# Expert routing tables of a state-space/mixture-of-experts kernel: part of their making moved into the convolution, the sums on two column positions of TensorE

## The chip, the cores and the metric

The kernel runs on one core of a Trainium2 chip. The metric is the device time of one launch in microseconds (us), the median of the runs. Engines: TensorE (PE, matmuls and its weight loads PEld), VectorE (DVE), ScalarE (ACT), GpSimd (POOL), and SyncE (SP), which here only issues DMAs.

## The reference

`x` has 32 sequences of 64 channels and 1024 time steps. A state-space convolution along time (its kernel made from `log_dt`, `C`, `A`; a skip `D`; a length mask) gives 2048 token rows of 1024 numbers. A mixture of 16 experts follows, two experts to a token, and its output is added to `x`:

```python
y = irfft(rfft(u * mask) * rfft(kernel))[..., :L] + u * mask * D   # then * mask
probs = softmax(y @ gate_w.T); vals, idx = top_k(probs, 2); vals /= vals.sum(-1)
h = silu(y @ g.T) * (y @ u.T)                  # 16 experts of 112
out = x + einsum('bei,hei,be->bh', h, d, w)    # w: vals at idx, else 0
```

All is fp32.

## The kernel before, in words

**Convolution.** The 64 channels are taken in 16 groups (`G`) of 4 (`HG`). For each group VectorE copies the new convolution kernel out of PSUM (`kernel_rows`), SyncE stores it to `k_rows` in DRAM and reads it back as Toeplitz matrices (L303, L312); TensorE runs 8 matmuls for each channel (`convolve_channel`, L939); VectorE reads each channel's result with the mask (`outputs`, L727) and transposes it to blocks (`block_rows`), and ScalarE issues the store of these as token rows of `y_rows` (`rows_out`). One group later TensorE makes the gate products on four column positions (`gates`, L950), ScalarE copies them (`partials`, L532), a matmul folds them to the logits of 128 tokens (`route`, L959), and VectorE copies these (`router`, L742). So a group is also a group of 128 tokens.

**Routing.** Every (choice k, group g) column of 128 tokens gets a slot in a list sorted by expert, in tiles of 128 slots. `choose` (L744) finds the two best experts of each token and one-hots of them, for 14 groups inside the last group of the convolution and for 2 behind it. Then two matmuls count tokens before and within the groups (L1023, L1024), VectorE scans them (L816), waits for ScalarE's exponentials (`spread_exp`), works out weights, tile starts and slots (L822 to L846), and in five `PIECES` the one-hot of a slot's tile (48 columns, `slot_hot`, L852) and of its row in the tile (128 columns, `slot_row`, L855). GpSimd multiplies the tile one-hot by the token's number and by its weight (L429, L432). TensorE sums 32 products `slot_row^T x [token part | weight part]` into one table (L1033: 128x128 against 96 columns). VectorE turns its first half into `from_row` (L860 to L862), the second into `slot_weight` (L864), and then works out each tile's expert (L866 to L875). `stay_awake` runs matmuls without use between these steps.

**Tiles.** GpSimd gathers 128 rows of `y_rows` per tile by `from_row` (L441; eight tiles ahead), then issues four empty scatters (L472). For each tile TensorE turns the rows (L1061), ScalarE and VectorE copy them, TensorE multiplies by gate and up weights (L1052), by the down weights (L1071), VectorE and ScalarE weigh the result (L906, L582), and GpSimd scatters it with addition into `out` (L456), which holds a copy of `x`. SyncE keeps six experts' weights in a ring: experts 0 to 2, then two pieces of the copy of `x`, then 3 to 5 are issued right behind the last Toeplitz loads; from 6 on as tiles finish.

Each engine runs its own queue in program order; semaphores order the engines.

Of the kernel before, what the change touches and what calls it, by code (L numbers as in the profile page):

```python
# [6 lines left out]
B, H, L = 32, 64, 1024  # L7
N = 64
P = 128
# [31 lines left out]
PIECES = ((0, 4), (4, 8), (8, 16), (16, 24), (24, K * G))  # L41
# [4 lines left out]
def build(nc, x_time, x_rows, lengths, params, skip, gate_t, gu_t, d_t, out):  # L46
# [4 lines left out]
    with ctx:  # L51
# [27 lines left out]
        at += 2 * HG * L - K * G * (P + 3 * MC)  # L79
        slot_row = flat[:, at:at + K * G * P].rearrange("p (j r) -> p j r", j=K * G)  # L80
        at += K * G * P
        slot_tile = flat[:, at:at + 2 * K * G * MC].rearrange("p (j n) -> p j n", j=K * G)
        at += 2 * K * G * MC
        slot_hot = flat[:, at:at + K * G * MC].rearrange("p (j n) -> p j n", j=K * G)
        par = sb("par", [P, 5, H])
# [46 lines left out]
        not_first = sb("not_first", [P, E, G])  # L132
        run = sb("run", [P, E, G])
# [3 lines left out]
        dest = sb("dest", [P, E, G])  # L137
        slot = sb("slot", [P, K * G])
# [16 lines left out]
        ys_of = [ys[:, s, :] for s in range(RY - R)] + [ys_more[:, s, :] for s in range(R)]  # L155
# [6 lines left out]
        k_bank = pb("k_bank", [P, HG, LO])  # L162
        k_ps = k_bank[0:LO, :, :]
        later_ps = conv_ps[:, 0, 0:E * G].rearrange("p (e g) -> p e g", e=E)
        count_ps = conv_ps[:, 1, 0:E * G].rearrange("p (e g) -> p e g", e=E)
        table_ps = conv_ps[:, 2, 0:2 * MC]
# [58 lines left out]
        hot_row_made = sem("hot_row_made")  # L225
        hot_weight_made = sem("hot_weight_made")
        hot_token_made = sem("hot_token_made")
        sources_made = sem("sources_made")
        table_made = sem("table_made")
# [42 lines left out]
        def _(sp):  # L272
# [66 lines left out]
        def _(pool):  # L339
# [68 lines left out]
            link(nc.gpsimd.memset(not_first[:, :, :], 1.0))  # L408
            nc.gpsimd.memset(not_first[:, :, 0:1], 0.0).then_inc(starts_marked, 1)
# [15 lines left out]
            weights = weight[:, :, :].rearrange("p k g -> p (k g)")  # L425
            for q, (lo, hi) in enumerate(PIECES):
                js = slice(lo, hi)
                pool.wait_ge(hot_made, q + 1)
                nc.gpsimd.tensor_tensor(slot_tile[:, js, 0:MC], slot_hot[:, js, :],  # L429
                                        token_no[:, js].unsqueeze(2).to_broadcast([P, hi - lo, MC]),  # L430
                                        ALU.mult).then_inc(hot_token_made, 1)
                nc.gpsimd.tensor_tensor(slot_tile[:, js, MC:], slot_hot[:, js, :],  # L432
                                        weights[:, js].unsqueeze(2).to_broadcast([P, hi - lo, MC]),
                                        ALU.mult).then_inc(hot_weight_made, 1)

# [28 lines left out]
            pool.wait_ge(ys_cleared, 2)  # L464
            for t in range(RY):
                gather(t)
# [31 lines left out]
        def _(act):  # L498
# [57 lines left out]

# [4 lines left out]

            nc.scalar.activation(silu[:, 0, 0:1], len_f[:, 0:1], ACT.Silu)

# [35 lines left out]
        def _(dve):  # L599
# [119 lines left out]
            def outputs(g, p, first):  # L719
# [5 lines left out]
                for h in range(HG):  # L725
                    dve.wait_ge(conv_done, g * HG + h + 1)
                    nc.vector.tensor_tensor(y_t[:, p, h, :, :],  # L727
                                            conv_ps[:, h, 0:C * B].rearrange("p (c b) -> p c b", c=C),
                                            mask_t[:, :, :], ALU.mult).then_inc(conv_read, 1)

# [13 lines left out]
            def choose(lo, hi):  # L744

                for g in range(lo, hi):
                    nc.vector.max(top_v[:, g, :], logits[:, g, :]).then_inc(top_found, 1)
                dve.wait_ge(top_found, hi)
                for g in range(lo, hi):
                    nc.vector.max_index(top_i[:, g, :], top_v[:, g, :], logits[:, g, :]).then_inc(top_made, 1)  # L750
                dve.wait_ge(top_made, hi)
# [8 lines left out]

                tt(spread[:, lo:hi, :], logits[:, lo:hi, :], top_v[:, lo:hi, 0:1].to_broadcast([P, n, E]), ALU.subtract)
# [3 lines left out]


# [22 lines left out]
            with dve.Fori(1, (G - 4) // 2) as i:  # L789
                for p in range(2):  # L790
# [4 lines left out]
                    angles(2 * i + 4 + p, p, False)  # L795
            for g in range(G - 4, G):
                if g + 2 < G:
                    kernel_rows(g + 2, g % 2, (g + 2) // 2, False)
                if g == G - 1:

                    dve.wait_ge(log_made, G - 2)
                    choose(0, G - 2)
                outputs(g, g % 2, False)
# [7 lines left out]
            choose(G - 2, G)  # L811
            block_rows(G - 1, (G - 1) % 2, (G - 1) // 2, False)

            dve.wait_ge(starts_marked, 1)
            dve.wait_ge(counted, 1)
            link(nc.vector.tensor_tensor_scan(run[:, :, :].rearrange("p e g -> p (e g)"),  # L816
                                              not_first[:, :, :].rearrange("p e g -> p (e g)"),
                                              conv_ps[:, 1, 0:E * G], 0.0, ALU.mult, ALU.add))


            dve.wait_ge(spread_exp, 1)
            links(vec.tensor_scalar(tiles[:, :], run[:, :, G - 1], 1.0 / P, HALF_DOWN, ALU.mult, ALU.add),  # L822
                  vec.reduce_sum(total[:, :], spread[:, :, :], AX.X))
            links(vec.tensor_scalar(tiles[:, :], tiles[:, :], ROUND, ROUND, ALU.add, ALU.subtract),
                  vec.reciprocal(total[:, :], total[:, :]))
            links(vec.tensor_scalar(tiles[:, :], tiles[:, :], 1.0, None, ALU.max, ALU.bypass),
                  vec.tensor_tensor(weight[:, :, :], top2[:, :, :], total[:, :].unsqueeze(1).to_broadcast([P, K, G]),
                                    ALU.mult))
            links(vec.tensor_tensor_scan(ends[:, :], ones[:, 0:E], tiles[:, :], 0.0, ALU.mult, ALU.add),
                  vec.tensor_tensor(norm[:, :], weight[:, 0, :], weight[:, 1, :], ALU.add))  # L830
            vec.tensor_copy(ends_i[:, :], ends[:, :]).then_inc(ends_made, 1)
            links(vec.tensor_tensor(starts[:, :], ends[:, :], tiles[:, :], ALU.subtract),
                  vec.reciprocal(norm[:, :], norm[:, :]))


            links(vec.tensor_tensor(weight[:, :, :], weight[:, :, :], norm[:, :].unsqueeze(1).to_broadcast([P, K, G]),
                                    ALU.mult),
                  vec.tensor_tensor(dest[:, :, :], run[:, :, :], later_ps, ALU.add))
            stt(dest[:, :, :], starts[:, :].unsqueeze(2).to_broadcast([P, E, G]), float(P), dest[:, :, :],
                ALU.mult, ALU.add)  # L840
            links(*[nc.vector.tensor_tensor(chosen[:, k, :, :], chosen[:, k, :, :],
                                            dest[:, :, :].rearrange("p e g -> p g e"), ALU.mult) for k in range(K)])
            link(nc.vector.reduce_sum(slot[:, :], chosen[:, :, :, :].rearrange("p k g e -> p (k g) e"), AX.X))
            ts(slot_q[:, :], slot[:, :], 1.0 / P, -HALF_DOWN, ALU.mult, ALU.add)
            ts(slot_q[:, :], slot_q[:, :], ROUND, ROUND, ALU.add, ALU.subtract)
            stt(slot[:, :], slot_q[:, :], -float(P), slot[:, :], ALU.mult, ALU.add)  # L846


            for q, (lo, hi) in enumerate(PIECES):
                js = slice(lo, hi)  # L850
                col = [P, hi - lo, MC]
                nc.vector.tensor_tensor(slot_hot[:, js, :], slot_q[:, js].unsqueeze(2).to_broadcast(col),  # L852
                                        iota_row[:, 0:MC].unsqueeze(1).to_broadcast(col),
                                        ALU.is_equal).then_inc(hot_made, 1)
                nc.vector.tensor_tensor(slot_row[:, js, :], slot[:, js].unsqueeze(2).to_broadcast([P, hi - lo, P]),  # L855
# [275 lines left out]
```

## Time and profile before

| | us |
|---|---|
| median of 3 runs (lowest, highest) | 499.8 (499.45, 500.56) |
| the profiled execution | 496.27 |
| its span, first to last instruction | 494.2 |
| TensorE busy | 435.8 (88%) |
| VectorE / ScalarE / GpSimd busy | 195.8 / 100.9 / 177.6 |

The span in 40 equal slices of 12.4 us; a digit is the busy share in tenths, PEclk the granted clock of TensorE in tenths of full speed, DMA the mean share of 16 DMA engines:

```profile
PE   0359999989999998895969999999999999999991
...
DVE  6924344333444432639613333333333333333330
ACT  3870000000001000011012222222222232222220
POOL 4542332222222200005685334446344354552322
PEclk9989999999999999997899999999999999999997
DMA  8966898989889998899584897997997796775541
```

The first 17 slices are the convolution, slices 18 to 20 (counted from 1) the routing, the rest the tiles. How to read it: an engine's share over the whole span mixes these stages; what counts for the change is what ended each wait in the middle one.

### The profile page before, as it was taken

The page shows a single profiled execution, that of the slowest core. Times are in us where ns is not written, and L with a number is a line of the kernel's source. Part 1 is how long each engine was busy: PE and PEld are TensorE (multiplying, and loading weights), DVE is VectorE, ACT ScalarE, POOL GpSimd, SP SyncE. Part 2 cuts the span into 40 slices and gives each one's busy share as a digit, 9 for nine tenths or more (in the row PEclk, how much of TensorE's full clock was granted, in tenths as well). Part 3 has the DMA queues.
Part 4 walks back from the last instruction along what each step waited for, and adds up shares of the span by engine and source line. Part 5 has one row for each costly group of instructions (what it writes and reads, how often), then busy time and mean ns, then how long its engine had stood idle before and what let it go on. Part 6 is the DMA issues. An engine that isn't in the chain of part 4 may idle for free.

```text
span 494.2 us, 9023 instructions
## 1 busy us (share of the span) xinstructions
PE 435.8 (88%) x2834; PEld 381.2 (77%) x2834; DVE 195.8 (40%) x512; ACT 100.9 (20%) x229; POOL 177.6 (36%) x217
## 2 busy tenths in 40 slices
PE   0359999989999998895969999999999999999991
PEld 0359998879899898884958887888887788888770
DVE  6924344333444432639613333333333333333330
ACT  3870000000001000011012222222222232222220
POOL 4542332222222200005685334446344354552322
PEclk9989999999999999997899999999999999999997
DMA  8966898989889998899584897997997796775541
GB/s 282 341 204 191 283 265 269 287 261 276 279 284 304 306 295 261 284 387 350 151 299 86 261 285 169 277 273 205 285 250 209 213 278 154 152 159 97 86 71 20
DMA packets 46490, 115.98 MB, mean 235 GB/s; under 512 B 10098, under 2 KB 25714, under 8 KB 46322
## 3 DMA queue, kind: packets, MB, share of 16 engines
q1 hardware_dynamic: 25138, 73.49, 45.5%
q0 software_dynamic: 12096, 33.58, 29.8%
q10 hardware_dynamic: 9216, 8.39, 5.5%
q8 instruction: 23, 0.38, 0.3%
q14 instruction: 17, 0.14, 0.1%
HBM read 93.63 MB, written 40.66 MB: 272 GB/s over the span
## 4 chain that ended last, share of the span: by engine, by line
PE 58%; DMA 23%; SPq 6%; DVE 6%; issue 2%; POOL 2%; ACT 0%; another core or an unknown queue 0%; ACTq 0%; POOLq 0%; DVEq 0%
PE conv_ps L1052 25%; DMA k_rows<-k_sb 17%; PE conv_ps L1071 14%; PE conv_ps L939 9%; PE turn_ps L1061 7%; DMA arena<-k_rows 4%; SPq L312 4%; SPq L311 3%; PE conv_ps L1033 2%; DVE tmp L622 1%; DMA ys<-y_rows,from_row 1%; PE conv_ps L1078 1%; POOL arena L429 1%; PE turn_ps L950 1%; DMA out<-arena,from_row 1%
## 5 line engine op out<-in xcount | busy, mean ns | idle before, releaser
L939 PE MATMUL conv_ps<-arena 128*128 128x256 f32 (+7 forms) x1024 | 157.1, 310 | 12.7 <-DMA arena<-k_rows 12.3
L939 PEld LDWEIGHTS conv_ps<-arena 128*128 128x128 f32 x1024 | 148.8, 192 | 20.6 <-issue 8.5
L1052 PE MATMUL conv_ps<-arena,ys_t 128*128 x640 | 127.8, 353 | 3.8 <-DVE ys_t L886 3.8
L1052 PEld LDWEIGHTS conv_ps<-arena,ys_t 128*128 128x128 f32 x640 | 118.1, 190 | 15.5 <-issue 15.5
L456 POOL DMA_INDIRECT out<-arena,from_row x40 | 62.9, 1572 | 119.9 <-DMA out<-arena,from_row 82.3
L1071 PE MATMUL conv_ps<-arena,hid_t 112*128 x160 | 75.7, 595 | 1.0 <-DVE hid_t L901 1.0
L727 DVE TENSOR_TENSOR arena<-conv_ps,mask_t 128x256 f32<-128x256 f32 x64 | 27.0, 424 | 98.6 <-PE conv_ps L939 97.7
L894 DVE TENSOR_TENSOR hid<-silu,conv_ps 128x112 f32<-128x112 f32 x40 | 10.9, 272 | 102.1 <-ACT silu L576 98.4
L906 DVE TENSOR_SCALAR arena<-conv_ps,slot_weight 128x512 f32<-128x512 f32 x40 | 30.0, 751 | 42.7 <-PE conv_ps L1071 41.7
L385 POOL TENSOR_TENSOR am<-wave,cs_re 128x128 f32<-128x128 f32 x16 | 6.5, 406 | 108.8 <-ACT wave L518 105.4
L1071 PEld LDWEIGHTS conv_ps<-arena,hid_t 112*128 112x128 f32 x160 | 27.2, 190 | 21.0 <-issue 20.8
L582 ACT ACTIVATE arena<-conv_ps,slot_weight 128x512 f32<-128x512 f32 x40 | 27.5, 688 | 47.3 <-PE conv_ps L1071 46.2
L886 DVE COPY ys_t<-turn_ps 128x512 f32<-128x512 f32 x40 | 27.7, 692 | 16.6 <-PE turn_ps L1061 13.4
L569 ACT COPY ys_t<-turn_ps 128x512 f32<-128x512 f32 x40 | 23.4, 586 | 51.4 <-PE turn_ps L1061 47.0
L576 ACT ACTIVATE silu<-conv_ps 128x112 f32<-128x112 f32 x40 | 10.6, 264 | 100.5 <-PE conv_ps L1052 98.1
L518 ACT ACTIVATE wave<-angle 128x384 f32<-128x384 f32 x16 | 8.2, 521 | 109.2 <-DVE angle L672 109.2
L429 POOL TENSOR_TENSOR arena<-arena,token_no 128x384 f32<-128x384 f32 (+1 forms) x5 | 7.3, 1451 | 54.5 <-DVE arena L852 54.5
L988 PE MATMUL turn_ps<-ones 128*128 128x128 f32 x50 | 7.6, 313 | 20.0 <-DVE cs_im L707 20.0
L441 POOL DMA_INDIRECT ys<-y_rows,from_row x20 | 21.3, 1064 | 9.7 <-issue 5.8
L441 POOL DMA_INDIRECT arena<-y_rows,from_row x20 | 21.0, 1050 | 6.1 <-issue 6.1
L1061 PE MATMUL turn_ps<-ident,ys 128*128 128x128 f32 x160 | 20.8, 273 | 1.8 <-DMA ys<-y_rows,from_row 1.8
L988 PEld LDWEIGHTS turn_ps<-ones 128*128 128x128 f32 x50 | 6.9, 222 | 20.0 <-issue 19.9
(149 smaller groups left out, 369.6 us busy)
## 6 DMA issues: line engine op xcount, KB each, us to landing
arena<-k_rows SPq DMA_DIRECT2D x64, 512.0 KB, 6.6
arena<-gu_t SPq DMA_DIRECT2D x16, 896.0 KB
y_rows<-y_blk ACTq DMA_DIRECT2D x64, 128.0 KB, 3.1
arena<-x_time SPq DMA_DIRECT2D x56, 128.0 KB, 5.3
arena<-d_t SPq DMA_DIRECT2D x16, 448.0 KB
arena<-x_time SPq DMA_DIRECT2D x2, 512.0 KB, 6.0
out<-arena,from_row POOLq DMA_INDIRECT x44
out<-ys SPq DMA_DIRECT2D x1, 512.0 KB, 7.4
```

The source lines that it names most:

```text
L312: sp.dma_start(toep[:, p, h, :], bass.AP(k_rows, (g * HG + h) * KROW, [[1, P], [1, L]])).then_inc(toep_in[p][h], 16)
L441: nc.gpsimd.indirect_dma_start(out=ys_of[t % RY], out_offset=None, in_=y_rows, in_offset=bass.IndirectOffsetOnAxis(ap=from_row[:, t:t + 1] ...
L456: nc.gpsimd.indirect_dma_start(out=out, out_offset=bass.IndirectOffsetOnAxis(ap=from_row[:, t:t + 1], axis=0), in_=od[:, t % R, :], in_off ...
L569: nc.scalar.copy(ys_t[:, t % 2, 0:C // 2, :], ytr_ps[:, 0:L // 2].rearrange("p (c n) -> p c n", n=P)).then_inc(yst_act, 1)
L582: nc.scalar.mul(od[:, t % R, 0:L // 2], down_ps[:, 0, :], slot_weight[:, t:t + 1]).then_inc(od_act, 1)
L727: nc.vector.tensor_tensor(y_t[:, p, h, :, :], conv_ps[:, h, 0:C * B].rearrange("p (c b) -> p c b", c=C), mask_t[:, :, :], ALU.mult).then_i ...
L886: nc.vector.tensor_copy(ys_t[:, t % 2, C // 2:, :], ytr_ps[:, L // 2:].rearrange("p (c n) -> p c n", n=P)).then_inc(yst_dve, 1)
L906: nc.vector.tensor_scalar(od[:, t % R, L // 2:], down_ps[:, 1, :], slot_weight[:, t:t + 1], None, ALU.mult, ALU.bypass).then_inc(od_dve, 1)
L939: last = nc.tensor.matmul(conv_ps[:, h, d * B:C * B], toep[:, p, h, d * P:(d + 1) * P], u_t[:, p, h, 0:(C - d) * B], start=(d == 0), stop= ...
L1052: last = nc.tensor.matmul(gu_ps, ys_t[:, t % 2, c, :], flat[:, bass.ds(bufs[t] * WE + c * GU, GU)], start=(c == 0), stop=(c == C - 1))
L1061: last = nc.tensor.transpose(ytr_ps[:, c * P:(c + 1) * P], ys_of[t % RY][:, c * P:(c + 1) * P], ident[:, :])
L1071: last = nc.tensor.matmul(down_ps[:, n, :], hid_t[:, t % 2, :], flat[0:INTER, bass.ds(bufs[t] * WE + C * GU + n * (L // 2), L // 2)], star ...
```

## The change

Groups 0 to 11 (`GA` = 12) are handled apart from groups 12 to 15 (`GB` = 4). What happens to the early ones goes between the channels of the last three groups of the convolution. A slot is now split: the rank of a token among its expert's tokens gives the row in the tile without the tile starts; the tile is the start plus the quotient of the rank.

Row one-hots of the early groups are multiplied by the token number by ScalarE (`token_rows`), ahead of and behind the last `partials`. Each table is summed as `tile one-hot^T x row one-hot`, 48 columns of weights against 128 columns, even columns at position 0 and odd ones at 64, copied by ScalarE to `halves`, and folded and turned by one matmul. There are two tables, one behind the other: tokens (with `from_row` and the first four gathers right behind) and weights. `slot_row` now lies in the buffers of gathered tiles 4 to 7, `row_token` over weights of experts 3 to 5, whose loads go behind the token table. The exponentials move ahead of the last `rows_out`, the weights behind the slots.

```diff
-            sp.wait_ge(factors_made, G)
-            load_expert(3)
-            load_expert(4)
-            sp.wait_ge(conv_done, G * HG)
-            load_expert(5)
-            for e in range(WB):
-                sp.wait_ge(w_in[e % WB], 32)
+            for e in range(3):
+                sp.wait_ge(w_in[e], 32)
+                sp.sem_inc(weights_ready, 1)
+            sp.wait_ge(tokens_out, 1)
+            for e in range(3, WB):
+                load_expert(e)
+            for e in range(3, WB):
+                sp.wait_ge(w_in[e], 32)
                 sp.sem_inc(weights_ready, 1)
...
+            pool.wait_ge(hot_made, 2 * K)
+            for k in range(K):
+                js = slice(k * G + GA, (k + 1) * G)
+                nc.gpsimd.tensor_tensor(hot_token[:, k * GB:(k + 1) * GB, :], slot_hot[:, js, :],
+                                        token_no[:, js].unsqueeze(2).to_broadcast([P, GB, MC]),
+                                        ALU.mult).then_inc(late_tokens, 1)
...
-            for t in range(RY):
+            for t in range(R):
+                gather(t)
+            pool.wait_ge(weights_out, 1)
+            for t in range(R, RY):
                 gather(t)
...
+            def token_rows(q):
+                k, lo = q // 2, (q % 2) * HALF
+                act.wait_ge(rows_made, q + 1)
+                for j in range(k * G + lo, k * G + lo + HALF):
+                    last = nc.scalar.mul(row_token[:, j, :], slot_row[:, j, :], token_no[:, j:j + 1])
+                last.then_inc(row_tokens, 1)
...
+            act.wait_ge(factors_made, G)
+            for q in range(3):
+                token_rows(q)
             partials(G - 1, (G - 1) % 2, False)
-            rows_out(G - 1, (G - 1) % 2)
+            token_rows(3)
             act.wait_ge(spread_made, 2)
...
+            rows_out(G - 1, (G - 1) % 2)
...
+            for n in range(2):
+                act.wait_ge(halves_summed[n], 1)
+                for part in (slice(0, MC), slice(P // 2, P // 2 + MC)):
+                    nc.scalar.copy(halves[part, n, :], halves_ps[n][part, :]).then_inc(halves_copied[n], 1)
...
+            between = {
+                G - 4: (None,) * HG,
+                G - 3: (lambda: best(0, GA), lambda: best_at(0, HALF), lambda: best_at(HALF, GA), None),
+                G - 2: (lambda: choose(0, GA), lambda: spreads(0, GA), None, None),
+                G - 1: (early_ranks, early_rows, more_rows, None),
+            }
...
+            rows_of(1, HALF, GA)
             router(G - 1, (G - 1) % 2)
...
+            for k in range(K):
+                hot_of(k, 0, GA)
+            for k in range(K):
+                hot_of(k, GA, G)
+            for k in range(K):
+                rows_of(k, GA, G)
+            dve.wait_ge(spread_exp, 1)
...
+            dve.wait_ge(tokens_out, 1)
...
+            for k in range(K):
+                js = slice(k * G, (k + 1) * G)
+                vec.tensor_tensor(hot_weight[:, js, :], slot_hot[:, js, :],
+                                  weights[:, js].unsqueeze(2).to_broadcast([P, G, MC]), ALU.mult).then_inc(weighted, 1)
...
+            dve.wait_ge(weights_out, 1)
+            nc.vector.tensor_copy(slot_weight[:, :], weight_ps).then_inc(lists_made, 1)
...
+                    if h == 3 and counting:
+                        pe.wait_ge(chosen_made, 1)
+                        pe.wait_ge(k_copied, G)
+                        count_tokens(later_a, count_a, slice(0, GA))
...
+            pe.wait_ge(ranks_begun, 1)
+            stay_awake(6, k_bank[:, 0:P])
             pe.wait_ge(chosen_made, 2)
+            count_tokens(later_b, count_b, slice(GA, G))
+            stay_awake(29, k_bank[:, 0:P])
+            def half_table(n, j, hot, row, first, last):
+                part = slice((j % 2) * (P // 2), (j % 2) * (P // 2) + MC)
+                return nc.tensor.matmul(halves_ps[n][part, :], hot, row, start=first, stop=last)
+            for n, (j, late) in enumerate(COLS):
+                if late:
+                    pe.wait_ge(late_tokens, j // G + 1)
+                    pe.wait_ge(rows_made, 2 * K + j // G + 1)
+                    hot, row = hot_token[:, (j // G) * GB + j % G - GA, :], slot_row[:, j, :]
+                else:
+                    pe.wait_ge(hot_made, j // G + 1)
+                    pe.wait_ge(row_tokens, 2 * (j // G) + (j % G) // HALF + 1)
+                    hot, row = slot_hot[:, j, :], row_token[:, j, :]
+                last = half_table(0, j, hot, row, n < 2, n >= last_two)
+            last.then_inc(halves_summed[0], 1)
+            stay_awake(2, k_bank[:, 0:P])
+            pe.wait_ge(halves_copied[0], 2)
+            nc.tensor.matmul(token_ps, halves[:, 0, :], fold_tiles[:, :], start=True, stop=True).then_inc(tokens_out, 1)
+            stay_awake(4, k_bank[:, 0:P])
+            for j in range(K * G):
+                pe.wait_ge(weighted, j // G + 1)
+                last = half_table(1, j, hot_weight[:, j, :], slot_row[:, j, :], j < 2, j >= last_two)
+            last.then_inc(halves_summed[1], 1)
+            pe.wait_ge(halves_copied[1], 2)
+            nc.tensor.matmul(weight_ps, halves[:, 1, :], fold_tiles[:, :], start=True, stop=True).then_inc(weights_out, 1)
+            stay_awake(4, k_bank[:, 0:P])
```

In order, the pieces are of SyncE, GpSimd (two), ScalarE (three), VectorE (four) and TensorE. `COLS` names the 24 early columns first. `early_ranks` scans the early counts and multiplies them with the chosen one-hots, `early_rows` reduces these to ranks, takes them modulo 128 and makes the first six row one-hots (`rows_of`), `more_rows` twelve more. GpSimd also makes `fold_tiles` and clears `halves` and two masks at the start of the kernel.

## Rows read from the trace of the kernel before

**Rows 1.** Chain of waits, 213 to 270: start us, length us, what.

```profile
213.26 0.43 DVE arena L727
...
220.38 1.28 ACT L559
...
234.35 7.55 PE conv_ps L1033 x48
...
242.41 0.20 DVE from_row L862
...
243.57 4.59 DMA ys<-y_rows,from_row
...
248.21 1.11 PE turn_ps L1061 x8
...
254.20 2.25 another core or an unknown queue
...
267.32 1.72 PE conv_ps L1071 x4
```

**Rows 2.** Stage windows: length, busy us (instructions) of each engine, PEclk, DMA share, GB/s.

```profile
230.00:232.00 2.00, 2.00 (x10) 2.00 (x11) 2.00 (x3) 0.00 (x0) 2.00 (x3) 0.50 1.02 345
...
255.00:260.00 5.00, 2.58 (x14) 2.58 (x15) 0.89 (x2) 0.59 (x1) 4.08 (x4) 1.00 0.65 252
```

**Rows 3.** TensorE's timeline: start, busy us, line; records are two a matmul.

```profile
202.92 2.48 PE L939 MATMUL conv_ps<-arena 128*128 128x256 f32 x16 [1.55 <-DMA arena<-k_rows]
...
213.74 0.65 PE L950 MATMUL turn_ps<-arena,gate_w 128*32 128x128 f32 x16 [0.52 <-DVE arena L727]
...
217.89 6.86 PE L988 MATMUL k_bank<-ones 128*128 128x128 f32 x60
229.79 3.70 PE L1033 MATMUL conv_ps<-arena 128*128 128x96 f32 x16 [5.05 <-POOL arena L432]
```

**Rows 4.** GpSimd's timeline: its first factors, and one product with token numbers.

```profile
19.89 0.40 POOL L385 TENSOR_TENSOR am<-wave,cs_re 128x128 f32<-128x128 f32 x1 [3.47 <-DVE cs_im L707]
...
229.66 0.95 POOL L429 TENSOR_TENSOR arena<-arena,token_no 128x192 f32<-128x192 f32 x1
```

**Rows 5.** ScalarE: timeline, and its group of scaled 512-column copies on the page.

```profile
14.34 7.74 ACT L502 ACTIVATE arena<-steps,decay 128x64 f32<-128x64 f32 x32
...
214.45 0.27 ACT L532 COPY parts<-turn_ps 128x128 f32<-128x128 f32 x1 [8.13 <-PE turn_ps L950]
...
L582 ACT ACTIVATE arena<-conv_ps,slot_weight 128x512 f32<-128x512 f32 x40 | 27.5, 688 | 47.3 <-PE conv_ps L1071 46.2
```

**Rows 6.** VectorE's timeline, 203 to 243.

```profile
203.21 1.17 DVE L747 MAX8 top_v<-logits 128x8 f32<-128x16 f32 x14
...
215.20 0.18 DVE L742 COPY logits<-turn_ps 128x16 f32<-128x16 f32 x1 [1.43 <-PE turn_ps L959]
...
218.23 0.65 DVE L816 TENSOR_TENSOR_SCAN run<-not_first,conv_ps 128x256 f32<-128x256 f32 x1
222.32 0.17 DVE L822 TENSOR_SCALAR tiles<-run 128x16 f32<-128x16 f32 x1 [3.44 <-ACT top L560]
...
226.41 0.69 DVE L843 TENSOR_REDUCE slot<-chosen 128x32 f32<-128x512 f32 x1
...
228.07 0.68 DVE L855 TENSOR_TENSOR arena<-slot,iota_row 128x512 f32<-128x512 f32 x1
...
229.25 0.99 DVE L855 TENSOR_TENSOR arena<-slot,iota_row 128x512 f32<-128x512 f32 x1
...
242.76 0.95 DVE L616 TENSOR_TENSOR passed<-iota_row,ends 128x768 f32<-128x768 f32 x1
```

**Rows 7.** DMA queues in 232 to 234, then 245 to 258: packets, MB, share.

```profile
q1 hardware_dynamic: 129, 0.62, 84.5%
q10 hardware_dynamic: 127, 0.11, 19.4%
...
q0 software_dynamic: 1187, 4.01, 87.4%
```

More of the change, by code:

```diff
@@ L40 @@
 SPANS = ((0, USUAL), (USUAL, USUAL + 4), (USUAL + 4, MT))
-PIECES = ((0, 4), (4, 8), (8, 16), (16, 24), (24, K * G))
+GA = G - 4
+GB = G - GA
+HALF = GA // 2
+COLS = tuple((k * G + g, 0) for k in range(K) for g in range(GA)) + tuple(
+    (k * G + g, 1) for k in range(K) for g in range(GA, G))
 NONE = 4 * K * TOK
@@ L154, in build @@
         ys = sb("ys", [P, RY - R, L])
-        ys_of = [ys[:, s, :] for s in range(RY - R)] + [ys_more[:, s, :] for s in range(R)]
+        slot_row = ys[:, :, :].rearrange("p s n -> p (s n)").rearrange("p (j r) -> p j r", j=K * G)
+        ys_of = [ys_more[:, s, :] for s in range(R)] + [ys[:, s, :] for s in range(RY - R)]
         ys_t = sb("ys_t", [P, 2, C, P])
@@ L717, in kernel_rows, with outputs @@
                                         ALU.add).then_inc(k_added, 1)
-            def outputs(g, p, first):
+            def outputs(g, p, first, between=(None,) * HG):
                 if not first:
@@ L806, in _ @@
                 router(g - 1, (g - 1) % 2)
+            rows_of(1, HALF, GA)
             router(G - 1, (G - 1) % 2)
             dve.wait_ge(log_made, G)
-            choose(G - 2, G)
+            best(GA, G)
+            best_at(GA, G)
+            choose(GA, G)
+            spreads(GA, G)
             block_rows(G - 1, (G - 1) % 2, (G - 1) // 2, False)
[L814 to L818, printed above, removed]
@@ L821, in _ @@
-            dve.wait_ge(spread_exp, 1)
-            links(vec.tensor_scalar(tiles[:, :], run[:, :, G - 1], 1.0 / P, HALF_DOWN, ALU.mult, ALU.add),
-                  vec.reduce_sum(total[:, :], spread[:, :, :], AX.X))
+            dve.wait_ge(counted, 2)
+            link(vec.tensor_tensor_scan(run_b[:, :, :].rearrange("p e g -> p (e g)"),
+                                        not_first_b[:, :, :].rearrange("p e g -> p (e g)"),
+                                        count_b, 0.0, ALU.mult, ALU.add))
@@ L836, in _ @@
+            link(vec.reciprocal(norm[:, :], norm[:, :]))
             links(vec.tensor_tensor(weight[:, :, :], weight[:, :, :], norm[:, :].unsqueeze(1).to_broadcast([P, K, G]),
                                     ALU.mult),
[L838 to L855, printed above, removed]
-                                        iota_row[:, :].unsqueeze(1).to_broadcast([P, hi - lo, P]),
-                                        ALU.is_equal).then_inc(hot_row_made, 1)
@@ L974, in convolve_first, with count_tokens, convolve @@
                         route(0, 0, True)
-            def convolve(g, p, i, second=False):
+            def count_tokens(later, count, groups):
+                nc.tensor.matmul(later, not_before[:, :], both[:, :, groups], start=True, stop=True)
+                nc.tensor.matmul(count, ones[:, :], both[:, :, groups], start=True, stop=True).then_inc(counted, 1)
+            def convolve(g, p, i, second=False, counting=False):
                 for h in range(HG):
+                    if h == 3 and counting:
+                        pe.wait_ge(chosen_made, 1)
+                        pe.wait_ge(k_copied, G)
+                        count_tokens(later_a, count_a, slice(0, GA))
                     pe.wait_ge(toep_in[p][h], 32 * i + 16)
@@ L1012, in _ @@
             for g in range(G - 4, G):
-                convolve(g, g % 2, g // 2)
+                convolve(g, g % 2, g // 2, counting=g == G - 2)
                 if g + 3 < G:
```

178 lines of the change are left out of this document (117 added, 61 removed).

## The prediction

> **What bounds the kernel now.** I read the chain of waits first. Between the convolution and the expert tiles it leaves TensorE's useful work: the last convolution result is read at 213.26, the first gathered tile is turned at 248.21, and from there to the end the chain is one 5.73 us tile after another (down projection at 261.59, then 267.32) [rows 1]. So 34.95 us lie in the routing stretch, and whatever brings the turn at 248.21 forward comes off the end, as long as the tiles keep their pace. The chain's pieces there are the exponentials (table load at 220.38), the table matmuls (234.35, 7.55 us for 24 of the 32), the cast of the sources (242.41) and the first gather (243.57, landing in 4.59 us). After it there is one odd piece, 2.25 us at 254.20 that the profile ascribes to nothing it knows. Then the stage windows: in 230 to 232 the granted clock is 0.50, the 1.2 GHz level, so the table matmuls run at half speed; TensorE had waited 5.05 us before them [rows 2, 3]. In 255 to 260 it is busy for 2.58 of 5 us and the clock is 1.00 [rows 2].
>
> **Part 1: the work put into the convolution.** Counting 12 groups on TensorE adds two matmuls over 192 columns before the last channel of group 14, some 0.7 us. Group 15 then waits 1.55 us for its Toeplitz rows anyway [rows 3], so I cost it at nothing; without that cover it costs its 0.7. VectorE gets the best-two search in group 13, the choice in group 14, and ranks and row one-hots between the channels of group 15. Each gap there is about 2 us and the pieces are 0.9 to 2.2 us, so the last channel is still read at 213.7, with little left over. The new memsets and the fold on GpSimd (about 0.8 us) lie in a 3.47 us wait before its first factors [rows 4].
>
> ScalarE is the exception. It gets 24 scaled copies of 128x128, and 18 of them stand in its queue ahead of the last group's copy of the gate partials, which now runs at 214.45 after 8.13 us of idleness [rows 5]. The nearest row has 32 of 128x64 in 7.74 us, 0.242 each; 512 columns take 0.688 alone [rows 5]. For 128 columns that bounds one between 0.242 and 0.40; I take 0.30. Row one-hots are ready from about 210.9 (the second channel's result at 208.4, its read 0.4, a reduce 0.5, three small steps 0.6, a one-hot of 768 elements 0.95 as [rows 6]). 18 x 0.30 = 5.4 gives 216.3, so the partials, their matmul and the last logits come **1.85 us later** (0.8 to 3.7), at 217.05 instead of 215.20.
>
> **Part 2: from the last logits to the slots.** Before, logits to scan took 3.03 us (215.20 to 218.23) for two groups; four groups cost two more max and four more index instructions (14 max take 1.17 us) and wider compares, together 0.5: scan at 220.6 [rows 6]. Behind the scan VectorE stood 3.44 us for the exponentials [rows 6]; with the weights moved back this goes. What is late next is VectorE itself: the scan over 64 elements 0.3, ten small steps at about 0.22 with their gaps 2.2, a product over 512 elements 0.75 (nearest the 0.68 one), a reduce 0.72, an add 0.2, that is 4.2. Tiles of all slots are known at 224.8; before, the first one-hot pair was being built from 227.8.
>
> **Part 3: the token table.** The one-hots of the early groups take 0.75 and 0.65, the late ones 0.6 together, then GpSimd's two late products at 0.95 [rows 4] end near 228.7. TensorE meanwhile runs 29 warming matmuls behind the late count (219.9): 30 took 6.86 us, 0.229 each [rows 3], so until 226.5, and no idle gap is longer than about 2.2 us; I take 1.00 for the clock. One 128-column matmul over the full array costs 0.229. Over narrow column positions the trace has only the gates: 8 matmuls of 128x32 by 128 columns on four positions in 0.65 us, 0.08 each [rows 3]. For two positions the bounds are 0.08 and 0.229; I take half of the full one with some loss, **0.125**, so 32 cost 4.0 and the sum is complete at 230.5. Two copies by ScalarE 0.5 and the fold matmul 0.3: tokens at 231.3. Three VectorE steps 0.65: sources at 231.95, against 242.6 before [rows 1]. The 10 us are about 7.1 from the tables at full clock on two positions without waiting for GpSimd's 32 products, and the rest from the earlier slots.
>
> The Trainium skill (TensorEngine Tiling (Array Packing), Tiling Modes, Key Properties) says that a change of tiling mode drains TensorE, while tiles of one mode run independently. Its second half agrees with the gates' 0.08 against 0.229 [rows 3]. The new tables change the mode a few times, not per matmul; by the rule two positions give at best half of 0.229, 3.7 us a table, 0.3 under my sum.
>
> **Part 4: gather, weights, first turn.** From the cast to the gather's landing took 1.16 + 4.59 us [rows 1]. New on the way is company: the loads of experts 3 to 5 (3 x 1.34 MB) now go out at 231.3, just ahead of the gathers. Two queues with work shared by packet: 129 against 127 packets in 2 us, 0.73 MB in all [rows 7]. A gather's packets are 4 KB, so it gets near half, 0.17 MB/us; alone the eight gathers ran at 4.01 MB in 13 us, 0.31 MB/us, the first far under that [rows 7]. I add 0.3 (bounds 0 and 4.6, a doubling): landing near 238. The output rows of group 15 go out 2.3 us later than before, but the loads that they shared the queues with until about 236 are gone; I cost them at nothing, at worst 3.
>
> Weights: their chain on VectorE (2.5 us from 228) is done before 231.3, so hidden. Two products over 768 elements follow the sources (0.95 each), TensorE's second table 4.0 from 232.95, copies and fold 0.8, the copy of the weights 0.2: 238.0. ScalarE waits for that before it turns a tile, and TensorE runs four more warming matmuls behind its fold: 237.75 + 0.9 = 238.65. So the weights, not the gather, decide, and the first turn is at **238.7 instead of 248.21: 9.5 us earlier**.
>
> Added waits behind: GpSimd holds gathers 4 to 7 and the four empty scatters until the second fold; tile 4 needs its gather 23 us after the first turn. The empty scatters stand behind 4.1 MB of gathers and beside 4.1 MB of loads: 8.2 MB at 0.36 MB/us from 233.3 end near 256.3. The first weighted tile waits for the first of them and must be written before the second down projection, 19.1 us after the first turn (267.32 - 248.21), 257.8. That holds narrowly, at no cost; if the odd 2.25 us do not return, it costs about 1.7 of them.
>
> Sum on the profiled execution: 496.27 - 9.5 = 486.8. The median of the runs shown is 3.5 above that execution; the same 9.5 off it gives **490.3**.
>
> **Rivals.**
> A. *The table matmuls stay as slow as they are* (the side that loses). Before, 24 cost 7.55, 0.314 each [rows 1], most of it at half clock. If the clock falls in the new waits for copies, or positions don't overlap, each table costs 10.05 instead of 4.0 and, as there are two in sequence now, 12.1 are lost: 2.6 slower, 502.4. It decides from 0.125 + 9.5/64 = 0.273 us per matmul. For it: 0.50 after 5.05 us of waiting. Against it: 1.00 in 255 to 260 despite 2.84 us of idleness before the second tile [rows 2, 3].
> B. *The positions run one after the other at full clock*: 0.229, 3.3 more per table, 6.7 in all: 497. Against it: the gates' 0.08.
> C. *Gathers behind the moved loads.* If the first gather doubles, or the empty scatters land 4 us later than worked out, 3 to 4 are given back: 494. The Trainium skill (DMA: Bandwidth & Descriptors, Queues, rings and completion order) has each DMA engine take turns between queues by packet; the trace agrees (129 and 127). By it the gather is slowed, never starved.
> D. *The odd 2.25 us vanish* and ScalarE's copies run at 0.242 (1.1 less): 9.5 + 0.6 to 3.3 earlier, 487 to 490.
> E. *The early work doesn't fit* between the channels and pushes the last read back by 1 to 2: 492.
>
> **How the numbers follow.** Forecast 0.50 (488.5 to 492.5), D 0.16, C 0.14, E 0.04, B 0.08, A 0.08. A measurement of this kernel can tell about 0.2%, 1 us, from no change. Faster: all but A, and a tail of C and B, 0.87; within 0.2%: 0.04; slower: 0.09. The range takes D whole with the table at 0.08 per matmul (1.4 each): 486; on the other side C and most of E, short of B: 496.
>
> **What would show it.** Right: the partials' copy near 216.3; no wait between scan and tiles; clock 1.00 through both tables and each about 4 us; the first turn near 239 with tiles still 5.73 us apart. Wrong: tables over 8 us (A), 128x48 matmuls at 0.229 (B), a turn waiting for its gather or a down projection for an empty scatter (C).

## The result, and the profile after

The changed kernel takes 493.86 us (median of 4 runs, 493.08 to 494.46) against 499.62 (4 runs, 497.25 to 500.56) on the same chip: ratio 0.9891 [0.9853, 0.9928]. That is 5.8 us less; 9.5 were forecast, to 490.3, and the range of 486 to 496 holds the time. A second timing of the same kernel (E5 below) gave 0.9928 [0.9895, 0.9962], 3.6 us less.

The two profiled executions differ by much less: 494.46 (span 492.7) against 496.27 (span 494.2). One execution of each is a thin basis here, so I divide every span at the same three places: C, the start of the last group's gate products; T, the first turn of a gathered tile; G3, the third tile's gate and up products, from where the tiles keep a steady pace.

| kernel, one execution each | C | T - C | G3 - C | span - G3 | span |
|---|---|---|---|---|---|
| before | 213.74 | 34.47 | 49.52 | 230.94 | 494.2 |
| before again (E1) | 213.89 | 35.11 | 53.30 | 230.71 | 497.9 |
| after | 211.65 | 33.04 | 49.93 | 231.12 | 492.7 |
| after again (E5) | 210.96 | 30.88 | 46.54 | 231.40 | 488.9 |

The tile stage (span - G3) did not change. The stretch from C to the third tile takes 51.4 us without and 48.2 with the change, as means of two, and the two of a kind differ by 3.8 and 3.4 us. C itself lay between 209.3 and 214.4 in the nine profiles that contain the change, and between 211.4 and 213.9 in the three that don't.

The chain of waits of the changed kernel, 198 to 270 (start us, length us, what), answers to [rows 1]:

```profile
211.09 3.31 ACT arena L580 x11
...
218.44 8.75 PE k_bank L1115 x58
227.19 3.65 PE conv_ps L1158 x64
...
232.69 0.20 DVE from_row L974
...
233.85 10.80 DMA arena<-y_rows,from_row
...
247.64 6.28 PE conv_ps L1200 x16
...
255.75 3.29 PE conv_ps L1200 x16
```

The exponentials are gone from the chain, and a whole table of 32 matmuls costs 3.65 where 7.55 stood for 24 of them. Three pieces have taken the place of what left: 8.75 us of warming matmuls (58 records, 29 matmuls), a gather that lands 10.80 us after its issue, and a first tile of 6.28 where the second has 3.29.

The page's row of granted clocks, 40 slices, shows two dents in the middle (slice 18, and slices 20 and 21) where the page of before has one (19 and 20):

```profile
PEclk9999999999999999979779999999999999999997
```

TensorE's timeline (start, busy us, line; in brackets the idle time before and what ended it) answers to [rows 3]:

```profile
211.65 0.65 PE L1068 MATMUL turn_ps<-arena,gate_w 128*32 128x128 f32 x16 [0.52 <-DVE arena L771]
214.60 0.40 PE L1077 MATMUL turn_ps<-fold,parts 128*128 128x16 f32 x2 [2.31 <-ACT parts L558]
214.85 1.73 PE L1115 MATMUL k_bank<-ones 128*128 128x128 f32 x12
218.23 8.96 PE L1115 MATMUL k_bank<-ones 128*128 128x128 f32 x58
...
233.79 3.70 PE L1158 MATMUL conv_ps<-ys,arena 128*48 128x128 f32 x64 [0.90 <-DVE arena L980]
240.12 0.66 PE L1183 MATMUL conv_ps<-fold_tiles,halves 128*128 128x48 f32 x2 [2.63 <-ACT halves L606]
...
244.69 1.97 PE L1209 MATMUL turn_ps<-ident,arena 128*128 128x128 f32 x8 [2.07 <-DMA arena<-y_rows,from_row]
```

And its windows (length, busy us of each engine, granted clock, DMA share, GB/s) answer to [rows 2]:

```profile
216.00:218.00 2.00, 1.26 (x7) 0.96 (x7) 1.86 (x12) 1.97 (x5) 0.00 (x0) 0.54 1.00 309
218.00:220.00 2.00, 2.00 (x11) 2.00 (x11) 1.78 (x8) 0.16 (x2) 0.00 (x0) 0.50 1.45 462
...
234.00:238.00 4.00, 3.49 (x64) 3.24 (x60) 2.82 (x9) 0.00 (x0) 3.39 (x3) 1.00 1.02 351
...
240.00:242.00 2.00, 1.88 (x9) 1.88 (x10) 0.56 (x4) 0.07 (x1) 0.42 (x1) 0.51 1.03 319
```

TensorE waits 2.31 us for ScalarE's copy and 0.74 more ahead of 217.32; then the clock is 0.54 and 0.50, the 1.2 GHz level, and the warming matmuls, meant to bridge the time to the table, last to 227.2 while their results are wanted by nobody. The tables themselves run at 1.00: 32 matmuls in 3.70 us, 0.115 each. From 240 the clock is low again, behind 2.63 us in which TensorE waits for the copies of the second table.

ScalarE's timeline answers to [rows 5]:

```profile
209.03 5.37 ACT L580 ACTIVATE arena<-ys,token_no 128x128 f32<-128x128 f32 x18 [4.81 <-DVE ys L835]
214.30 0.25 ACT L558 COPY parts<-turn_ps 128x128 f32<-128x128 f32 x1
...
239.53 0.54 ACT L606 COPY halves<-conv_ps 48x128 f32<-48x128 f32 x2 [8.06 <-remote]
```

The 18 copies take 0.298 each and hold the partials back to 214.30, C + 2.65; before, it was C + 0.71. The last line starts 2.04 us after the second table's end (233.79 + 3.70).

VectorE, which answers to [rows 6]: behind the scan stands no wait any more.

```profile
218.65 0.25 DVE L921 TENSOR_TENSOR_SCAN run_b<-not_first_b,conv_ps 128x64 f32<-128x64 f32 x1
...
219.19 0.18 DVE L925 TENSOR_SCALAR tiles<-run_b 128x16 f32<-128x16 f32 x1
...
222.80 0.19 DVE L660 TENSOR_TENSOR slot_q<-tile_off,rank_q 128x32 f32<-128x32 f32 x1
```

The DMA queues in 234 to 238, then in 239 to 245 (packets, MB, share), answer to [rows 7]; q0 is the gathers, q1 the loads of experts 3 to 5, issued from 231.97:

```profile
q1 hardware_dynamic: 273, 1.40, 101.4%
...
q1 hardware_dynamic: 246, 1.20, 59.4%
q0 software_dynamic: 216, 0.82, 42.3%
```

The gather is issued at 233.85, but in 234 to 238 there is no line of q0 at all; its first packet runs 5.9 us after the issue, where the kernel before had 1.9. Once its packets run, the queues share nearly one to one.

### The profile page after: what moved, and what is told of

Same layout as the page of the kernel before. It is cut to its first block, busy times and chain, and to the rows that moved or that the text cites. A ratio compares the mean times of both kernels' runs of the same rounds, so it can differ in the third digit from the quotient of the medians.

```text
span 492.7 us, 9187 instructions
## 1 busy us (share of the span) xinstructions
PE 437.4 (89%) x2880; PEld 381.5 (77%) x2880; DVE 196.3 (40%) x525; ACT 108.9 (22%) x257; POOL 168.8 (34%) x213
## 4 chain that ended last, share of the span: by engine, by line
PE 72%; DMA 13%; DVE 5%; ACT 3%; SPq 2%; issue 2%; POOL 1%; POOLq 0%; DVEq 0%; ACTq 0%
PE conv_ps L1200 25%; PE conv_ps L1057 20%; PE conv_ps L1219 14%; PE turn_ps L1209 7%; DMA k_rows<-k_sb 6%; DMA arena<-k_rows 4%; DMA arena<-y_rows,from_row 2%; PE k_bank L1115 2%; PE turn_ps L1068 1%; DVE tmp L666 1%; ACT arena L528 1%; ACT arena L580 1%; SPq L336 1%; PE conv_ps L1226 1%; SPq L335 1%
## 5 line engine op out<-in xcount | busy, mean ns | idle before, releaser
L1200 PE MATMUL conv_ps<-arena,ys_t 128*128 x640 | 130.8, 358 | 1.9 <-DVE ys_t L1004 1.9
L1200 PEld LDWEIGHTS conv_ps<-arena,ys_t 128*128 128x128 f32 x640 | 120.4, 194 | 14.2 <-issue 13.7
L1209 PE MATMUL turn_ps<-ident,arena 128*128 128x128 f32 x160 | 21.7, 280 | 2.1 <-DMA arena<-y_rows,from_row 2.1
L1209 PEld LDWEIGHTS turn_ps<-ident,arena 128*128 128x128 f32 x160 | 19.5, 146 | 3.4 <-DMA arena<-y_rows,from_row 2.4
```

The lines of the kernel that those rows point to most:

```text
L1200: last = nc.tensor.matmul(gu_ps, ys_t[:, t % 2, c, :], flat[:, bass.ds(bufs[t] * WE + c * GU, GU)], start=(c == 0), stop=(c == C - 1))
L1209: last = nc.tensor.transpose(ytr_ps[:, c * P:(c + 1) * P], ys_of[t % RY][:, c * P:(c + 1) * P], ident[:, :])
```

## The experiments

Twelve profiles stand behind this; those below ran in three sets, E1 to E4, E5 to E8, and E9 with E10, each on one chip beside runs of the kernel before.

**E1, the kernel before once more, unchanged.**

> The kernel before, unchanged, for a second profile. The first profiled execution took 496.27 us, 3.3 less than the median of 499.6, and in the profiles the changed kernel gains only 1.8. Theory 1 (the missing time lies in the convolution, whose end moves with the DMAs): the last convolution result is read later than 213.3, at 215 to 217, and the stretch from there to the first full tile stays near 44.2. Rival (the routing stretch itself was lucky in the first profile): last read near 213, stretch 47 or more.

One execution, 499.97 us. The convolution ends where it did (C 213.89), so it isn't there that the first profile was short. The stretch behind it is: T - C is 35.11, and the second tile falls to half clock. One window, then TensorE's lines up to that tile:

```profile
260.00:262.00 2.00, 2.00 (x6) 1.82 (x6) 0.00 (x0) 0.00 (x0) 1.70 (x2) 0.50 0.04 1
```

```profile
256.51 0.32 PE L1078 MATMUL conv_ps<-ident,hid 128*112 128x128 f32 x1 [1.27 <-issue]
259.68 4.97 PE L1052 MATMUL conv_ps<-arena,ys_t 128*128 x16 [2.85 <-DVE ys_t L886]
```

In the profile that I forecast from, the clock was 1.00 there [rows 2], with nearly the same wait right before the tile:

```profile
257.42 3.29 PE L1052 MATMUL conv_ps<-arena,ys_t 128*128 x16 [2.84 <-DVE ys_t L886]
```

The program is the same, but here 1.27 us more of waiting lie just ahead, so the two executions don't show that an equal wait can end at either level. They do show that a clock read once behind a wait is not the program's property.

**E2, the loads of experts 3 to 5 behind the first four gathers.**

```diff
             sp.wait_ge(tokens_out, 1)
+            for t in range(R):
+                sp.wait_ge(gathered[t], 16)
             for e in range(3, WB):
```

> The changed kernel, but SyncE issues the loads of experts 3 to 5 only when the four early gathers have landed. Theory 1 (the first gather's 10.8 us, against 4.6 before, is the company of these loads): it lands within 5 us of its issue, the first turn comes 5 to 6 us earlier, the first tile is still at half clock or better; 486 to 489. Rival (the gather is late for its own indices or for the stores of the rows): landing stays near 10 us, time 493 to 495.

Ratio 0.994 [0.9895, 0.9984], 493.7 us. The gather's part held: its first packet runs 2.5 us after the issue at 232.90 (q0 in 234 to 238, next fence), and TensorE's first turn waits for no gather. T - C falls to 28.12.

```profile
q0 software_dynamic: 164, 0.61, 56.2%
```

```profile
239.61 1.04 PE L1211 MATMUL turn_ps<-ident,arena 128*128 128x128 f32 x8
...
248.36 4.87 PE L1202 MATMUL conv_ps<-arena,ys_t 128*128 x16 [2.46 <-DVE ys_t L1006]
```

The time, 486 to 489 by the expectation, did not follow the turn. The second tile waits 2.46 us, much as in the kernel before, and then runs mostly at half clock (0.55 in 248 to 250), and the first weighted tile waits for the first empty scatter, issued at 244.82 and landed 14.76 us later, now behind the loads (VectorE's line):

```profile
259.68 0.75 DVE L1026 TENSOR_SCALAR arena<-conv_ps,slot_weight 128x512 f32<-128x512 f32 x1 [4.85 <-DMA out<-arena,from_row]
```

**E3, more warming matmuls around the second fold**, 10 ahead of its wait and 18 instead of 4 behind it.

```diff
             last.then_inc(halves_summed[1], 1)
+            stay_awake(10, k_bank[:, 0:P])
             pe.wait_ge(halves_copied[1], 2)
...
-            stay_awake(4, k_bank[:, 0:P])
+            stay_awake(18, k_bank[:, 0:P])
```

> The changed kernel with ten warming matmuls in the wait for the copies of the second table and eighteen instead of four behind its fold. Theory 1 (the first tile runs at 1.2 GHz because TensorE waited twice before it): clock 1.00 at the first turn, its gate and up matmuls 3.3 instead of 6.3 us and the turn 1.1 instead of 2.0; 3 to 4 us less, 489.5 to 491. Rival (the first tile was slow for its operands): 6 us again, time within 1 us of 493.9.

490.74 us, ratio 0.9894 [0.9782, 1.0006]: the time alone decides nothing. The first turn is back at full speed (1.09), but the tile behind it is not:

```profile
241.09 1.09 PE L1210 MATMUL turn_ps<-ident,arena 128*128 128x128 f32 x8 [0.86 <-DMA arena<-y_rows,from_row]
243.16 4.97 PE L1201 MATMUL conv_ps<-arena,ys_t 128*128 x16 [0.98 <-DVE ys_t L1004]
```

So half of the theory held. The gather took 11.54 us to land here; it still ends the wait.

**E4, both tables on one column position.**

```diff
-                part = slice((j % 2) * (P // 2), (j % 2) * (P // 2) + MC)
+                part = slice(0, MC)
```

with one copy instead of two per table, and waits to match.

> The changed kernel with every column of a table at position 0 of TensorE, so one half and one copy. Theory 1 (two positions overlap): each table takes 32 x 0.229 = 7.3 instead of 3.7 us, sources 3.3 later, and as the gather decides, the end 3 to 4 later: 497 to 498. Rival (the matmuls are bound by weight loads or the one-hots): tables under 5 us, time within 1 us of 493.9.

The second table takes 7.19 us instead of 3.70, 0.225 a matmul, and the first 7.2:

```profile
239.42 7.19 PE L1158 MATMUL conv_ps<-ys,arena 128*48 128x128 f32 x64 [0.89 <-DVE arena L980]
```

So the two positions do overlap, almost fully. Time: 495.02 us, ratio 0.9975 [0.9941, 1.001], no difference from before that can be told. The changed kernel itself wasn't timed in this set, so what the second position is worth in time stays open.

**E5, the changed kernel once more, unchanged**, for a base on this chip.

> The changed kernel, unchanged, beside the others on one chip. Its gate products of the last group began at 211.65 in the first profile, 2.1 earlier than in the kernel before (213.74), with nothing changed that reaches them. Theory 1 (that start moves with the DMAs from run to run): 209 to 215 again, unrelated to the edit; time over before 0.985 to 0.993. Rival (the change itself shortens the convolution): 211.7 or less again. The first gather lands about 10 us after its issue and the first tile's gate and up matmuls take about 6 us at 1.2 GHz in either case.

494.1 us, 0.9928 [0.9895, 0.9962]. The wait for the partials is 2.31 us again and the clock falls again, but it is back sooner (TensorE's timeline):

```profile
214.15 2.87 PE L1115 MATMUL k_bank<-ones 128*128 128x128 f32 x12
...
217.56 6.73 PE L1115 MATMUL k_bank<-ones 128*128 128x128 f32 x58
```

The 29 warming matmuls take 6.73 us here (8.96 in the first profile), the first tile 5.03 (6.28): both dents of the clock differ from one execution to the next. C came at 210.96, where the rival had it; E4 (214.35) and E10 (214.17) speak for theory 1.

**E6, only the first 6 of ScalarE's 24 scaled copies ahead of the partials**, 18 behind.

```diff
-            for q in range(3):
-                token_rows(q)
+            token_rows(0)
             partials(G - 1, (G - 1) % 2, False)
-            token_rows(3)
+            for q in range(1, 4):
+                token_rows(q)
```

> The changed kernel with ScalarE's copies of the one-hots 6 to 23 put behind the last group's partials, not ahead of 12 of them. Theory 1 (they hold up the last logits by 1.9 us, and TensorE's 2.3 us of waiting lowers its clock, so that the 29 warming matmuls take 9.0 instead of 6.6): no wait there, clock 1.00 from 214 to 226, the token table 2.5 to 4.3 us earlier after the gate products of the last group, and as much off the end: 489.5 to 491.5 if the kernel changed is at 493.9. Rival (the copies come late for the table instead): the table waits for them, less than 1 us gained.

488.62 us, 0.9826 [0.9776, 0.9877]: 5.5 us under E5 on the same chip. TensorE waits 0.39 us for the partials instead of 2.31, and the clock stays (its timeline, then a window):

```profile
210.35 0.40 PE L1077 MATMUL turn_ps<-fold,parts 128*128 128x16 f32 x2 [0.39 <-ACT parts L558]
...
213.57 6.69 PE L1115 MATMUL k_bank<-ones 128*128 128x128 f32 x58
```

```profile
216.00:218.00 2.00, 2.00 (x21) 2.00 (x20) 1.86 (x10) 1.97 (x4) 0.00 (x0) 1.00 1.13 458
```

The token table ends at C + 14.7, against C + 17.0 in E5 and C + 19.2 in the first profile. The gather is as late as ever (11.35 us to its landing), and the first tile is at 4.87. The profiles don't account for all of the 5.5 us: G3 - C is 44.67, 1.9 less than in E5's and 5.3 less than in the first, and C itself comes 1.6 earlier than in E5, which nothing shows to be the edit's doing.

**E7, joined:** E6, E2's waits, E3's 10 warming matmuls, and on GpSimd the empty scatters ahead of gathers 4 to 7.

```diff
-            for t in range(R, RY):
-                gather(t)
...
+            for t in range(R, RY):
+                gather(t)
```

> The changed kernel with four edits: those copies behind the partials; the loads of experts 3 to 5 behind the four early gathers; the four empty scatters ahead of gathers 4 to 7; ten warming matmuls in the wait for the second table's copies. Theory 1 (what was given back are these four): the first turn 28 to 29 us after... the gate products of the last group in the second experiment was 28.1; here 24.5 to 26, no wait for the empty scatters, 484 to 487 where the changed kernel has 493.9. Rival (each wait uncovers the next): 489 or more.

483.92 us, 0.9729 [0.9673, 0.9785], under both kernels. The first turn comes at C + 25.27, and both first tiles run at full clock:

```profile
234.81 1.04 PE L1211 MATMUL turn_ps<-ident,arena 128*128 128x128 f32 x8
236.83 3.29 PE L1202 MATMUL conv_ps<-arena,ys_t 128*128 x16 [0.98 <-DVE ys_t L1005]
...
241.97 3.29 PE L1202 MATMUL conv_ps<-arena,ys_t 128*128 x16 [0.87 <-DVE ys_t L1005]
```

E2's early wait for an empty scatter is gone. Part is given back all the same: from G3 to the end it takes 233.8 us, not 231.1. VectorE's waits in 250 to 480 (us, times, longest) have a line that the changed kernel has not; the first of its ten waits ends at 305, the other nine behind 350:

```profile
DVE arena L1025 <- DMA out<-arena,from_row: 31.5, 10, 4.8
```

**E8, the kernel before with one edit:** ScalarE's exponentials ahead of the last `rows_out`.

```diff
-            rows_out(G - 1, (G - 1) % 2)
             act.wait_ge(spread_made, 2)
...
+            rows_out(G - 1, (G - 1) % 2)
```

> The kernel before with ScalarE's two exponentials ahead of the stores of the last group's rows: this part of the change alone. Theory 1 (the 3.44 us wait of VectorE is for them and the rest of the chain follows): wait under 0.6 us, slots 2.9 to 3.3 us earlier, the end 2.5 to 3.5 earlier than the kernel before. Rival (the tables then wait longer for GpSimd's products or the stored rows come late for the gather): under 1 us.

494.46 us, 0.9942 [0.9902, 0.9982], beside E5's 0.9928 on the same chip. VectorE goes on behind its scan without the wait of 3.44 us [rows 6], and the table ends at C + 24.6 instead of C + 28.1:

```profile
215.85 0.65 DVE L816 TENSOR_TENSOR_SCAN run<-not_first,conv_ps 128x256 f32<-128x256 f32 x1
216.53 0.17 DVE L822 TENSOR_SCALAR tiles<-run 128x16 f32<-128x16 f32 x1
```

One moved line thus gives 2.9 us of the whole change's 3.6 there; the intervals overlap so far that only "a good part" is shown. The profiles agree: T - C is 30.68 (30.88 in E5) and G3 - C is 48.55, beside 48.2 with the whole change and 51.4 before, as means of two.

**E9, E7 with one gather instead of four between the two tables; E10, E7 again beside it.**

```diff
-            for t in range(R):
-                gather(t)
-
+            gather(0)
             pool.wait_ge(weights_out, 1)
+            for t in range(1, R):
+                gather(t)
```

> The joined kernel (e7) with only the first gather ahead of the weights; gathers 1 to 3 follow them, ahead of the empty scatters. In e7, as in four other profiles, ScalarE begins to copy the second table some 2 us after its last matmul, by a signal that the profile can't name. Theory 1 (TensorE's signal is held up while GpSimd issues the next gathers): the copy begins within 0.2 us of the table's end, weights 2 us earlier, the first turn then waits for the first gather's landing; 0 to 2 us off e7. Rival (it has nothing to do with them): 2.0 us late again, time as e7 or up to 2 later, as gather 1 lands later than its turn.

> The joined kernel (e7) unchanged, beside that on the same chip: 0.968 to 0.978 of the kernel before, the first turn 25.3 us after the gate products of the last group, both first tiles at clock 1.00.

E9 489.05 us, 0.9821 [0.9775, 0.9866]; E10 486.05, 0.9763 [0.9707, 0.9818]. In E9 ScalarE starts its copies 0.05 us after the second table (E9's TensorE line, then ScalarE's):

```profile
228.84 3.70 PE L1159 MATMUL conv_ps<-ys,arena 128*48 128x128 f32 x64 [0.89 <-DVE arena L981]
```

```profile
232.59 0.55 ACT L607 COPY halves<-conv_ps 48x128 f32<-48x128 f32 x2 [6.08 <-PE conv_ps L1159]
```

In E10 it is 1.26 us. The first turn gains nothing by it (C + 24.82 and C + 24.83): in both, the second fold comes only behind the ten warming matmuls, at C + 23.70 and C + 23.71, so the late signal is hidden there. In E9 VectorE waits 58.3 us for scatters in 250 to 480, against 33.6 in E10, and the tile stage takes 241.4 us, against 233.6; that the gathers, which now go later, push the scatters back is the likely cause, not one tested by itself. E7's order has the lowest median of those run, in E7 and in E10; the intervals of E9 and E10 overlap.

## Why the prediction was right in sign and too large

**What held.** Part 1: ScalarE's copies came at 0.298 (0.30 taken) and the partials 1.94 us later relative to C (1.85), and the early work didn't push the convolution's end back (rival E). Part 2: the wait of 3.44 us went, and the slots were known at C + 11.3 (C + 11.1). Part 3's price per matmul: 0.115 where 0.125 was taken, and E4 shows that it is by overlap, so rivals A and B are out as told. Rival D's first half came true as well: the odd 2.25 us did not return, and the second tile waits 0.87.

**What failed.** The time that came out, 493.86, is the one that rival C has (494, chance 0.14), but not by its sum: the gather cost more than told there, the clock fell, the odd wait went, and the two profiles differ by an earlier C that nobody forecast. That the stated range holds it is in part luck. The first turn was forecast at C + 25.0 and came at C + 33.04, 8.1 us later. Three terms make that up.

1. *The sources of the token table: +3.0, of which the clock 2.3.* The step was "no idle gap is longer than about 2.2 us; I take 1.00 for the clock". The gap was foreseen almost to size, 2.31 us and then 0.74; the clock behind it was not. It fell to 0.50, so 29 warming matmuls took 8.96 us and not 6.6, and the sources came at C + 21.24, not C + 18.21. The rest is small: the warming begins 0.4 later, the table is 0.3 shorter, and copies, fold and the three steps take 0.6 more. E6 takes the wait away, and the clock stays at 1.00. The row that I set against it, 1.00 in 255 to 260 behind 2.84 us [rows 2], was a single reading and no rule: E2's second tile ran at half clock behind 2.46. How much the fall costs is not fixed either: from the partials' fold to the table it took 12.5 us in the first profile, 10.3 in E5 with the same wait ahead, and 9.8 in E6 without it.

2. *"I add 0.3" for the gather's company: +5.7.* From the sources to the landing it took 0.96 + 10.80 us, not 6.05. That is rival C, beyond its price: 5.1 net of the next term, where 3 to 4 were told. I reasoned from two queues that were both running [rows 7], and so only from the sharing. Here three loads had been queued just before, and from the gather's issue to its first packet went 5.9 us; from there to the landing 4.9, where the kernel before has 1.9 and 2.7. So about two thirds of the loss is the late start, and a third the sharing. The start is the steadier of the two: 5.8 to 6.0 us in all five profiles with the loads ahead (the first, E3 to E6), 2.5 in the four with the loads behind (E2, E7, E9, E10), 1.9 in the three without the change. The Trainium skill (DMA: Bandwidth & Descriptors, Queues, rings and completion order) has each DMA engine take turns between the queues that it has work for. The trace agrees once the gather's packets run: 216 against 246 in 239 to 245. "Slowed, never starved" was my inference from that, and for the first 5.9 us it was wrong. E2 shows that the loads are the cause: with them behind, the turn waits for no gather.

3. *"So the weights, not the gather, decide": -0.65.* With the gather that late, the weights no longer counted. They were late too: in E2, where the gather is in time, the first turn still comes at C + 28.12, not C + 25.0.

Behind the turn more went, which the sum did not have at all. The clock fell again, at the 2.63 us wait for the second table's copies, and stayed low through the 2.07 us wait for the gather, so the first turn cost 1.97 and the first tile 6.28, 3.9 us over their pace at full clock. That ate what the vanished odd wait of the kernel before would have given (rival D, which I took as a gain only). So in the two first profiles G3 - C is the same within 0.4 us, and what they differ by is C. That C is really earlier with the change isn't settled: 211.4 in the mean of nine against 213.0 of three, with a scatter of 5 us.

E2 and E3 show how a wait that is taken away alone uncovers the next (the empty scatter, a second tile at half clock). Only E7, which takes them away together, has the forecast's first turn, at C + 25.3, and E9 and E10, which are built on it, at C + 24.8.

**How finely it can be measured.** I said 0.2%. Ten to twelve runs of one kernel gave intervals of 0.7 to 0.9%, and two profiled executions of the kernel before differ by 3.7 us. The sign is safe here (both timings exclude 1); a gain of 1 us would not have been seen.

**What stays open.** Why TensorE's end of the second table reaches ScalarE late (2.04 us after, 0.04 in E4, 0.05 in E9). It goes with GpSimd issuing gathers at that moment, in E2, E3, E5 to E7 and E10 too (1.25 to 2.06), and not in E4 and E9, where none is being issued; by what path wasn't tried. Why the clock holds behind one wait (2.84 us in the first profile of the kernel before) and falls behind another (2.46 in E2). Why a gather's first packet comes so late with loads queued ahead: that the loads do it is shown by E2, by what path is not.

## What to carry to other kernels

Work put into an engine's idle time is priced by what is queued behind it on that engine, and then by what idles for that: here 1.9 us of late partials also cost TensorE its clock, and putting the copies behind them gave 5.5 us (E6 against E5), of which the profiles account for 1.9 to 5.3. A bulk load does not go right ahead of the one small gather that everything waits for; it goes behind its landing, and what is queued after the load is checked next. Try the cheapest edit of a large change by itself (E8) and run each kernel's profile twice before reading a clock or a 2 us wait from it.

## What the runs showed of the hardware that I had not expected

- A gather issued while 4 MB of loads were being queued elsewhere (231.97 to 235.0) moved no packet for 5.9 us and landed after 10.80 us (11.54 in E3); with the loads behind it (E2) it was 2.5 us to the first packet, and in the kernel before 1.9, with 4.59 to the landing [rows 1].
- An empty scatter, which moves no row, took 14.76 us to its landing behind gathers and loads (E2).
- The second tile of one program ran at 1.00 in one execution and at 0.50 in another (E1, with 1.27 us more of waiting ahead); behind the same wait of 2.31 us, the changed kernel's warming matmuls took 8.96 us in one execution and 6.73 in another (E5).
- Two column positions of 48 weights each gave 0.115 us per matmul, one gave 0.225: the two overlap with hardly any loss.
